# Weight loads in four groups, and the five engine lists ordered anew, in a kernel that runs a one-layer vision tower on one core

## The chip, the core and the metric

The kernel runs on one core of a Trainium2 chip. A core has five engines that run their own instruction streams: TensorE (PE, matmuls; its weight loads are shown as PEld), VectorE (DVE), ScalarE (ACT), GpSimd (POOL), and SyncE (SP), which issues the transfers here. They meet only at semaphores. The metric is the device time of one launch in microseconds, which is the time for all 128 images.

## What is computed

For each of 128 images of 3x224x224: cut into 196 patches of 16x16, take the real part of each patch's 2-D FFT, weight it and project it to 192 numbers; add a class token and positions (197 tokens). Then two residual blocks: attention with 12 heads of 16, and attention with 12 heads of 64 whose queries and keys are normalised per head and whose heads are weighted by gates (2 shared heads, the best 2 of 10 routed heads).

```python
h = tok(x, freq_weight_h, freq_weight_w, proj_w, proj_b, cls_token, pos_emb)
h = h + attn(layernorm(h), Wq, bq, Wk, bk, Wv, bv, Wo, bo)
h = h + ffn(layernorm(h), qkv_w, qkv_b, q_norm_w, ..., wg_w, wg0_w, wg1_w, proj_w, proj_b)
# ffn:
q = layernorm(q, q_norm_w, q_norm_b); k = layernorm(k, k_norm_w, k_norm_b)
o = softmax((q * scale) @ k.T) @ v          # 12 heads of 64
o = masked_gates[..., None] * o
return o @ proj_w + proj_b
```

## The kernel before

An image is a chain of some 58 PE steps, each with its evacuations and pointwise work on DVE, ACT and POOL. The tokens lie in two chunks of 99 partitions. The steps are named in the lists of `ORDER` (lines 145 to 172):

- `tok`: the image, folded by the symmetry of the FFT (`fold`, `xhi`, `xlo` make an fp16 high and low part), times the effective token weights: 22 matmuls.
- `x1T`, `qk1_0..2`, `v1`, `s1_0..11`, `ctx0..2`, `wo`: first attention. `s1` on PE does four heads at once, in a block of 32 rows each; its entry in the list names four banks. `ctx` works in blocks of 32 columns.
- `x2T`, `qk0..5`, `v2_0..3`, `ms0..2`, `rstd0..5`: second attention's projections and head norms. `ms` (mean squares by a selection matrix) has blocks of 32 columns. On POOL, `sq` makes the squares and `bias` adds the norm's bias.
- `s2_0..11`: scores, two heads at once in blocks of 64 rows, fp32. DVE takes the row maxima (`nmax`), ACT the exponentials and their sums, DVE divides the gate by the sum (`gr`), POOL multiplies (`sc`), PE transposes (`pT`, fp32, full array), ACT copies the result, and `o2` multiplies with the values, two heads at once in blocks of 64 columns, fp32. `proj` is the last projection, 36 matmuls.

Each engine has a list of its own, written out by hand. An entry `3:s1_0@4135` reads: in iteration i do step s1_0 of image i+3, and put its results in PSUM banks 4, 1, 3 and 5. `run_phases` walks the list once per iteration, i from -4 to 127, and leaves out the steps of images that don't exist; the middle iterations are a hardware loop. An engine does its list strictly in order; a step that waits holds up everything behind it. A bank has one sequence of users, in the order of PE's list; a step waits (`room_for`) until the user before it has been read out.

Ahead of the lists stand the preparations. SP issues 29 loads of weights and constants, all on one semaphore `s_w` (lines 404 to 428). Many land in buffers that the images use later (`raw(p1, ...)`, `raw(pT, ...)`). DVE waits for all of them (line 824), scales the token weights (signal `s_pw` to PE, which makes the effective token weights in 24 matmuls, lines 533 to 538), subtracts the means of `wq` and `wk`, splits each weight into fp16 parts (`split`, lines 841 to 855), fills buffers (lines 859 to 877), scales PE's product (lines 879 to 885) and signals `s_const` (line 886). POOL waits for that and clears rows of `p1` and `pT` (lines 448 to 453); ACT and PE wait for POOL. Every DVE step here waits for the one before it (`link`).

Of the kernel before, what the change touches and what calls it, by code (L numbers as in the profile page):

```python
# [143 lines left out]

ORDER = {
    "pe": """
0:pT_1@1 0:pT_2@4 0:s2_8@35 2:ctx1@6 1:ms0@0 1:ms1 1:ms2 2:ctx2@2 0:pT_3@1 0:pT_4@7 0:pT_5@3 3:x1T@4 0:o2_0@6 0:o2_1@7
0:s2_10@21 0:pT_6@0 1:rstd0@4 1:rstd1@3 1:rstd2@5 3:qk1_0@6 0:pT_7@0 0:pT_8@4 1:s2_0@32 0:pT_9@7 2:wo@4 0:o2_2@0
0:o2_3@5 1:v2_0@1 1:rstd3@2 0:pT_10@7 0:pT_11@6 3:s1_0@4135 1:s2_2@02 0:o2_4@6 0:o2_5@7 1:v2_1@4 3:qk1_1@1 1:v2_2@3
1:v2_3@6 2:x2T@5 1:rstd4@3 4:tok@4 3:v1@0 3:s1_4@3257 2:qk0@1 2:qk1@0 2:qk2@4 2:qk3@1 3:qk1_2@6 1:rstd5@2 1:s2_4@43  # L150
3:ctx0@0 2:qk4@5 1:s2_6@12 1:pT_0@4 3:s1_8@5760 0:proj@3 2:qk5@7
""",
    "dve": """
1:s2_1 0:gr5 2:wo 0:ol2 0:ol3 1:v2_0 1:rstd3 3:s1_0 3:s1_1 3:s1_2 1:s2_2 3:s1_3 2:nx2 0:ol4 1:v2_1 1:v2_2 1:s2_3
3:qk1_1 1:v2_3 2:x2T 0:ol5 1:rstd4 4:tok 3:s1_4 1:gl 3:ctx0 3:s1_5 1:gate1 3:s1_6 1:gate2 1:gate3 1:gr0 3:s1_7 1:rstd5
1:s2_4 3:cl0 1:s2_5 3:qk1_2 1:gr1 1:s2_6 3:s1_8 3:s1_9 1:gr2 3:s1_10 3:s1_11 0:proj 1:s2_7 3:ctx1 3:ctx2 1:s2_8 4:nx1
1:gr3 1:s2_9 3:cl1 3:cl2 2:var2 1:gr4 4:x1T 1:ol0 1:s2_10 2:rstd0 1:ol1 2:rstd1 1:s2_11 4:qk1_0 2:rstd2 2:s2_0
""",
    "act": """
1:qk0 1:qk1 2:s1_5 1:qk2 2:s1_6 1:qk3 2:qk1_2 2:s1_7 2:ctx0 0:s2_4 1:qk4 0:s2_5 0:pT_0 2:s1_8 2:s1_9 0:s2_6 2:s1_10  # L160
2:s1_11 1:qk5 0:pT_1 0:s2_7 2:ctx1 0:pT_2 0:s2_8 1:var0 2:ctx2 0:pT_3 1:var1 0:pT_4 0:s2_9 3:x1T 0:pT_5 0:o2_0 0:pT_6
0:o2_1 0:s2_10 3:qk1_0 0:pT_7 0:pT_8 0:s2_11 1:s2_0 1:s2_1 0:pT_9 0:o2_2 0:o2_3 0:pT_10 0:pT_11 3:s1_0 3:s1_1 0:o2_4
3:s1_2 4:xhi 3:s1_3 3:qk1_1 0:o2_5 1:s2_2 2:x2T 1:s2_3 3:v1 3:s1_4 1:gate0
""",
    "pool": """
0:sc1 0:bias5 0:sc2 1:sq4 1:sq5 0:sc3 0:sc4 1:bias0 0:h2c 1:h2b 0:sc5 2:root2 1:bias1 4:fold 4:xlo 1:bias2 3:h1b
1:bias3 1:bias4 4:root1 2:sq0 2:sq1 1:sc0 2:sq2 2:sq3
""",
    "sp": """
4:load 0:store  # L170
# [31 lines left out]
def build_vit_block(nc, ins, out, images):  # L202
    with ExitStack() as ctx:
# [200 lines left out]
        loads = [*zip(basis, ("basis0", "basis1", "basis2")), (proj_tok, "proj_tok"), (freq_h[:], "freq_h"), (freq_w[:], "freq_w"),
                 (pos, "pos"), (tok_add, "tok_add"), (wq1_raw, "wq1"), (wk1_raw, "wk1"), (wv1_raw, "wv1"),
                 (wgate_raw, "wgate"), (wq_raw, "wq"), (wk_raw, "wk"), *zip(wv2_raw, ("wv2a", "wv2b")),
                 (ident[:], "ident"), (sel_var[:], "sel_var"), (sel_rstd[:], "sel_rstd"), (low_rows[:], "low_rows"), (weight_rows[:], "weight_rows"),
                 (bias_rows[:], "bias_rows"), (mask1[:], "mask1"), (wo1_raw, "wo1"), (bo1[:], "bo1"),
                 (ln_w[:], "ln_w"), (ln_b[:], "ln_b"), (wp2_raw, "wp2"), (bp2[:], "bp2")]
# [411 lines left out]
        def _(dve):  # L821
            V = nc.vector

            dve.wait_ge(s_w, 16 * len(loads))
# [11 lines left out]
            for x in (wq_raw, wk_raw):  # L836
                link(V.tensor_reduce(wqk_mean[:], x, op=ALU.add, axis=AX.X))
                link(V.tensor_scalar(wqk_mean[:], wqk_mean[:], 1.0 / E2, None, ALU.mult))
                link(V.tensor_tensor(x, x, wqk_mean[:].unsqueeze(3).to_broadcast([128, 3, H, E2]), op=ALU.subtract))
# [32 lines left out]
            for x in (mhalf,):  # L872
                link(V.memset(x[:], -0.5))
            link(V.memset(ones[:], 1.0))
            link(V.memset(gx[:], 2.0))
# [281 lines left out]
```

## Time and profile before

| | |
|---|---|
| median of 3 runs | 5231.84 us (5231.14 to 5232.46) |
| the profiled execution | 5229.47 us, its span 5227.7 us, mean granted clock 0.994 |
| busy, share of the span | PE 5089.4 us (97%), DVE 4644.1 (89%), ACT 4374.0 (84%), POOL 3438.4 (66%) |
| instructions | PE 61744 matmuls, DVE 14799, ACT 17537, POOL 3462 |
| bytes moved | 131.44 MB, a mean of 25 GB/s |
| the chain that ended last | PE 96% |

How to read it: busy time is the time in which an engine's instructions run, without semaphore and register work. Matmuls are pipelined: one begins before the one ahead has ended, and the times between their starts, not their durations, add up to the time of a step. The share of busy time is a mean over the start, the loop and the end. In a timeline, consecutive instructions of one kind are merged into a row: its first column is the start of the first of them, so the difference of the first columns of two rows is the time of everything from the one to the other.

### The profile page before, as it was taken

The numbers are of one execution on the slowest core, as the hardware profiler recorded it, in microseconds if no ns is written. First come the engines' busy times: TensorE is split into PE (matmuls) and PEld (weight loads), VectorE is DVE, ScalarE is ACT, GpSimd is POOL, SyncE is SP. The second block draws the span as 40 slices with busy tenths as digits, with TensorE's granted clock in tenths as the row PEclk, the third lists the DMA queues.
The fourth block names the chain that finished last, engine by engine and source line by source line (L and its number), as shares of the span: only waits on it lengthen the run. The fifth ranks groups of instructions, "written<-read, shape, count | busy, mean of one in ns | idle before, by whom it ended". The sixth has DMA issues, their size and how long they took to land.

```text
span 5227.7 us, 196546 instructions
## 1 busy us (share of the span) xinstructions
PE 5089.4 (97%) x61744; PEld 4233.4 (81%) x61744; DVE 4644.1 (89%) x14799; ACT 4374.0 (84%) x17537; POOL 3438.4 (66%) x3462
## 2 busy tenths in 40 slices
...
GB/s 83 21 24 29 22 22 23 28 22 22 29 22 22 29 22 22 29 22 22 23 28 22 22 29 22 22 29 22 22 29 22 22 23 28 22 22 29 22 23 8
DMA packets 69030, 131.44 MB, mean 25 GB/s; under 512 B 8628, under 2 KB 34624, under 8 KB 68704
## 3 DMA queue, kind: packets, MB, share of 16 engines
...
q14 instruction: 30, 0.25, 0.0%
...
## 4 chain that ended last, share of the span: by engine, by line
PE 96%; issue 2%; ACT 1%; DVE 1%; POOL 0%; POOLq 0%; ACTq 0%; DVEq 0%
PE bank L521 82%; PE bank L698 12%; PE bank L563 2%; ACT p L766 0%; ACT pq L804 0%; DVE nmax L939 0%; POOL pq L505 0%; ACT pT L810 0%; DVE nmax L1038 0%; DVE x L909 0%; DVE qkn L1033 0%; ACT qkc L778 0%; DVE qk L934 0%; DVE v L1015 0%; DVE stats L896 0%
## 5 line engine op out<-in xcount | busy, mean ns | idle before, releaser
L505 POOL TENSOR_TENSOR pq<-pq,gn 99x788 f32<-99x788 f32 x768 | 1152.5, 1501 | 747.3 <-DVE gn L1047 735.1
L766 ACT ACTIVATE p<-bank,nmax 99x197 f32<-99x197 f32 x3072 | 1289.3, 441 | 276.8 <-DVE nmax L939 276.8
L804 ACT ACTIVATE pq<-bank,nmax 99x197 f32<-99x197 f32 x3072 | 1330.0, 464 | 9.3 <-DVE nmax L1038 8.9
L810 ACT ACTIVATE pT<-bank 99x394 f32<-99x394 f32 x1536 | 764.2, 519 | 242.6 <-PE bank L698 242.6
L939 DVE TENSOR_REDUCE nmax<-bank 99x2 f32<-99x394 f32 x1536 | 820.5, 562 | 87.5 <-PE bank L521 59.3
L509 POOL TENSOR_TENSOR sq<-qkc 128x396 f32<-128x396 f32 x768 | 658.6, 872 | 318.4 <-ACT qkc L778 318.4
L1038 DVE TENSOR_REDUCE nmax<-bank 99x2 f32<-99x394 f32 x1536 | 849.4, 560 | 5.2 <-PE bank L521 5.2
L804 ACT ACTIVATION_READ_ACCUMULATOR pq<-bank,nmax 99x1 f32 x3072 | 752.7, 245 | 0.0
L521 PE MATMUL bank<-x2T,wqkc 128*128 128x198 f16 (+1 forms) x7680 | 742.3, 249 | 5.8 <-ACT p L766 4.9
L698 PE MATMUL bank<-ident,pq 99*99 99x99 f32 (+1 forms) x6144 | 723.1, 256 | 3.7 <-POOL pq L505 1.7
L698 PEld LDWEIGHTS bank<-ident,pq 99*99 99x99 f32 (+1 forms) x6144 | 606.2, 165 | 143.8 <-issue 139.8
L521 PEld LDWEIGHTS bank<-x2T,wqkc 128*128 128x128 f16 (+1 forms) x7680 | 646.5, 97 | 80.4 <-issue 41.1
L521 PE MATMUL bank<-qkb 64*99 64x197 f32 x6144 | 703.0, 347 | 5.2 <-issue 3.0
L514 POOL TENSOR_TENSOR qkb<-qkn,ln_b 128x396 f32<-128x396 f32 x768 | 645.1, 848 | 67.7 <-DVE qkn L1033 67.4
L766 ACT ACTIVATION_READ_ACCUMULATOR p<-bank,nmax 99x1 f32 x3072 | 676.6, 220 | 0.0
L521 PE MATMUL bank<-pT,v 128*64 128x197 f32 x6144 | 599.1, 336 | 1.0 <-ACT pT L810 0.9
L521 PEld LDWEIGHTS bank<-qkb 64*99 64x99 f32 x6144 | 451.2, 162 | 126.0 <-issue 83.9
L521 PEld LDWEIGHTS bank<-pT,v 128*64 128x64 f32 x6144 | 406.1, 136 | 116.8 <-issue 32.7
L521 PE MATMUL bank<-wv,x2T 128*99 128x384 f16 (+3 forms) x2560 | 497.6, 333 | 0.2 <-ACT p L766 0.2
L463 POOL TENSOR_TENSOR xl<-xa,xh 128x784 f16<-128x784 f32 x128 | 208.5, 1629 | 370.3 <-ACT xh L738 370.3
L1033 DVE TENSOR_TENSOR qkn<-bank,qkc 128x396 f32<-128x396 f32 x768 | 431.2, 562 | 5.9 <-PE bank L521 0.4
L521 PEld LDWEIGHTS bank<-wv,x2T 128*99 128x99 f16 (+1 forms) x2560 | 294.1, 125 | 146.8 <-issue 73.0
...
## 6 DMA issues: line engine op xcount, KB each, us to landing
xa<-in_xa SPq DMA_DIRECT2D x128, 392.0 KB, 3.1
xb<-in_xb SPq DMA_DIRECT2D x128, 392.0 KB, 3.7
out_tokens<-res SPq DMA_DIRECT2D x128, 74.2 KB
out_tokens<-res SPq DMA_DIRECT2D x128, 73.5 KB
...
```

Source lines behind the costliest of these rows:

```text
L463: nc.gpsimd.tensor_tensor(xl[:, :, 1:T], xa[:], xh[:, :, 1:T], op=ALU.subtract).then_inc(s_xl.up(), 1)
L505: nc.gpsimd.tensor_tensor(pair, pair, factor, op=ALU.mult).then_inc(s_sc.up(), 1)
L509: nc.gpsimd.tensor_tensor(sq[:, t], qkc[:, t], qkc[:, t], op=ALU.mult).then_inc(s_sq.up(), 1)
L514: nc.gpsimd.tensor_tensor(qkb[:, t], qkn[:, t % QKN_SLOTS], ln_b[:].unsqueeze(2).to_broadcast([128, 2, TP]), op=ALU.add).then_inc(s_qk.up( ...
L521: return nc.tensor.matmul(o, l, r, start=first, stop=last)
L698: last = nc.tensor.transpose(o[0:TC, k * T + c * TC:k * T + c * TC + n], pq[0:n, h % SLOTS, c, k * TC:k * TC + TC], ident[0:n, 0:n])
L766: last = nc.scalar.activation(p1[0:TC, h, c, :], psum("s1", h)[0:TC, c * T:c * T + T], ACT.Exp, bias=nmax1[:, c, h:h + 1], accum_out=sum1[ ...
L804: last = nc.scalar.activation(pq[0:TC, h % SLOTS, c, 0:T], psum("s2", h)[0:TC, c * T:c * T + T], ACT.Exp, bias=nmax2[:, h, c:c + 1], accum ...
L810: nc.scalar.activation(pT[0:TC, h].rearrange("p a b -> p (a b)"), psum("pT", h)[0:TC, 0:2 * T], ACT.Copy).then_inc(free("pT", h), 1)
L939: V.tensor_reduce(nmax1[:, :, h], psum("s1", h)[0:TC, 0:2 * T].rearrange("p (a b) -> p a b", a=2), op=ALU.max, axis=AX.X, negate=True).the ...
L1033: V.tensor_tensor(qkn[:, t % QKN_SLOTS].rearrange("p a b -> p (a b)"), psum("rstd", t)[:, 0:2 * TP], qkc[:, t].rearrange("p a b -> p (a b) ...
L1038: V.tensor_reduce(nmax2[:, h, :], psum("s2", h)[0:TC, 0:2 * T].rearrange("p (a b) -> p a b", a=2), op=ALU.max, axis=AX.X, negate=True).the ...
```

## The change

1. The 29 loads are issued in another order, in four groups with a semaphore each: for the token weights (8 loads: the bases, `proj_tok`, `freq_h`, `freq_w`, `bias_rows`, `mask1`), for the first attention (4: `wq1`, `wk1`, `wv1`, `wgate`), `wq` and `wk` (2), and all others (15). PE waits for the first group only.
2. DVE fills its buffers (all but `v2`) before it waits for any load, without a `link` between them. Then it waits for one group at a time: token weights, splits of the first attention's weights, means and splits of `wq` and `wk`, everything else.
3. The lists of all engines but SP are ordered anew. Each holds the same steps as before; positions, numbers of images ahead and banks differ. On PE `s2_8` and `s2_10` stand together, and so do `s2_4` and `s2_6`; `o2_2` and `o2_3` stand apart. The greatest number of images ahead is 4, as before.

The lists, after (those before are printed above):

```diff
     "pe": """
+2:s1_8@6725 0:o2_0@0 0:o2_1@1 0:rstd5@4 1:qk4@3 1:qk5@6 3:x1T@4 0:s2_8@72 0:s2_10@30 1:ms0@6 2:ctx1@5 1:ms1 1:ms2
+2:ctx2@7 0:pT_4@4 3:qk1_0@2 0:pT_5@5 0:pT_6@4 3:v1@1 1:rstd0@6 1:rstd1@3 0:o2_2@5 0:pT_7@6 0:pT_8@2 3:s1_0@4307
+0:o2_3@5 1:rstd2@6 0:pT_9@1 1:v2_0@2 2:wo@4 0:pT_10@3 0:pT_11@2 1:s2_0@61 0:o2_4@3 0:o2_5@0 1:rstd3@4 3:qk1_1@7
+3:qk1_2@5 1:v2_1@3 1:v2_2@4 1:rstd4@6 1:v2_3@1 2:x2T@7 1:s2_2@32 3:s1_4@4056 3:ctx0@1 2:qk0@7 2:qk1@3 2:qk2@4 4:tok@2
+1:s2_4@10 1:s2_6@75 2:qk3@4 1:pT_0@3 1:pT_1@6 0:proj@1 1:pT_2@0 1:pT_3@3
     "dve": """
+0:s2_11 1:var2 0:gr4 3:qk1_0 1:rstd0 2:cl2 1:rstd1 0:ol2 3:s1_0 3:s1_1 0:gr5 3:s1_2 3:s1_3 1:v2_0 1:rstd2 2:wo 0:ol3
+1:s2_0 3:ctx0 1:s2_1 1:rstd3 0:ol4 2:nx2 3:qk1_1 1:v2_1 1:v2_2 1:rstd4 3:qk1_2 0:ol5 1:v2_3 1:s2_2 2:x2T 3:s1_4 1:s2_3
+1:gl 3:s1_5 1:gate1 1:gate2 1:gate3 3:s1_6 3:cl0 1:gr0 3:s1_7 1:s2_4 1:s2_5 1:gr1 4:tok 1:s2_6 1:s2_7 4:nx1 1:gr2
+0:proj 3:s1_8 3:s1_9 3:s1_10 1:rstd5 3:s1_11 3:ctx1 1:ol0 1:s2_8 1:s2_9 4:x1T 3:ctx2 1:gr3 1:ol1 1:s2_10 3:cl1
     "act": """
+0:pT_2 0:pT_3 2:s1_8 2:s1_9 2:s1_10 0:o2_0 1:qk4 2:s1_11 1:qk5 0:o2_1 3:x1T 0:s2_8 0:s2_9 2:ctx1 1:var0 1:var1 0:pT_4
+0:s2_10 3:qk1_0 2:ctx2 0:pT_5 0:s2_11 3:v1 0:pT_6 0:o2_2 0:pT_7 0:pT_8 3:s1_0 0:o2_3 3:s1_1 3:s1_2 0:pT_9 0:pT_10
+0:pT_11 3:s1_3 0:o2_4 0:o2_5 1:s2_0 3:qk1_1 4:xhi 1:s2_1 3:qk1_2 2:x2T 1:s2_2 3:s1_4 3:ctx0 1:gate0 1:s2_3 2:qk0
+3:s1_5 2:qk1 3:s1_6 2:qk2 3:s1_7 1:s2_4 1:s2_5 1:pT_0 2:qk3 1:pT_1 1:s2_6 1:s2_7
     "pool": """
+0:sc4 1:h2b 1:bias0 1:bias1 0:sc5 4:fold 2:root2 4:xlo 3:h1b 1:bias2 1:bias3 1:bias4 2:sq0 2:sq1 1:sc0 1:sc1 4:root1
+1:sc2 2:sq2 2:sq3 1:bias5 2:sq4 1:h2c 2:sq5 1:sc3
```

The preparations, the core of the diff:

```diff
-            for dst, name in loads:
-                sp.dma_start(dst, ins[name]).then_inc(s_w, 16)
+            for dst, name in token_loads:
+                sp.dma_start(dst, ins[name]).then_inc(s_w0, 16)
...
+            for dst, name in last_loads:
+                sp.dma_start(dst, ins[name]).then_inc(s_w3, 16)
-            pe.wait_ge(s_w, 16 * len(loads))
+            pe.wait_ge(s_w0, 16 * len(token_loads))
             pe.wait_ge(s_pw, 1)
-            dve.wait_ge(s_w, 16 * len(loads))
+            V.memset(parts[0][:], 1.0)
+            V.memset(parts[1][:], 1.0)
+            for x in (vs1, ctxT, pq, oT, xh, xl):
+                V.memset(x[:], 0.0)
...
+            dve.wait_ge(s_w0, 16 * len(token_loads))
...
+            dve.wait_ge(s_w1, 16 * len(first_loads))
+            split(wq1_raw, wqk1[:, :, 0:384])
...
+            dve.wait_ge(s_w2, 16 * len(second_loads))
             for x in (wq_raw, wk_raw):
...
+            dve.wait_ge(s_w3, 16 * len(last_loads))
             for x, n, m in zip(wv2_raw, (0, 384), (384, 768)):
...
-            for x in (vs1, ctxT, pq, oT, v2, xh, xl):
-                link(V.memset(x[:], 0.0))
+            link(V.memset(v2[:], 0.0))
```

## Rows read from the trace of the kernel before

**Rows 1.** Windows: stretch, us, then busy us (instructions) by engine, clock, DMA share, GB/s.

```profile
2000.00:3000.00 1000.00, 998.52 (x12203) 831.56 (x12201) 907.14 (x2922) 863.59 (x3466) 678.74 (x685) 1.00 0.07 24
```

**Rows 2.** PE's timeline over one image: start us, us, engine, line, tiles, count.

```profile
2500.93 0.59 PE L698 MATMUL bank<-ident,pq 99*99 99x99 f32 x4
2501.36 0.67 PE L521 MATMUL bank<-rs_hl,sel_rstd 128*128 128x198 f16 x6
...
2502.74 0.86 PE L698 MATMUL bank<-ident,pq 99*99 99x99 f32 x8
2503.53 0.91 PE L521 MATMUL bank<-qkb 64*99 64x197 f32 x8
...
2505.89 1.56 PE L521 MATMUL bank<-pT,v 128*64 128x197 f32 x16
2507.38 1.02 PE L521 MATMUL bank<-wv,x2T 128*99 128x384 f16 x5
...
2508.41 0.86 PE L698 MATMUL bank<-ident,pq 99*99 99x99 f32 x8
2509.32 0.55 PE L521 MATMUL bank<-qk 32*99 32x197 f16 x16
...
2516.08 0.24 PE L521 MATMUL bank<-weff,xh 128*99 128x192 f16 x1
...
2517.81 0.25 PE L521 MATMUL bank<-weff,xl 128*99 128x192 f16 x1
...
2528.06 0.55 PE L521 MATMUL bank<-qk 32*99 32x197 f16 x16
2528.53 3.17 PE L521 MATMUL bank<-wp,oT 128*99 128x192 f16 x36
2531.54 1.03 PE L521 MATMUL bank<-x2T,wqkc 128*128 128x198 f16 x10
...
2536.53 1.29 PE L698 MATMUL bank<-ident,pq 99*99 99x99 f32 x12
2537.66 0.52 PE L563 MATMUL bank<-ident,parts 99*128 99x99 f16 x8
...
2539.59 0.91 PE L521 MATMUL bank<-qkb 64*99 64x197 f32 x8
2540.43 0.59 PE L698 MATMUL bank<-ident,pq 99*99 99x99 f32 x4
```

**Rows 3.** PE's timeline begun inside an o2 visit, at 2538.7 and at 2539.55.

```profile
2538.49 1.17 PE L521 MATMUL bank<-pT,v 128*64 128x197 f32 x12
...
2539.33 0.33 PE L521 MATMUL bank<-pT,v 128*64 128x197 f32 x2
```

**Rows 4.** ACT's timeline: the first softmax half of s1_8.

```profile
2529.23 0.43 ACT L766 ACTIVATE p<-bank,nmax 99x197 f32<-99x197 f32 x1 [0.51 <-DVE nmax L939]
```

**Rows 5.** Timeline of the start; in brackets the engine's idle time before and what ended it.

```profile
28.01 1.19 DVE L834 TENSOR_SCALAR pT<-pT,freq_h,freq_w 72x576 f32<-72x576 f32 x2 [28.01 <-DMA bp<-in_bp]
...
40.02 0.56 DVE L843 TENSOR_SCALAR wqk<-sq 128x768 f16<-128x768 f32 x1
...
54.20 0.56 DVE L843 TENSOR_SCALAR wv<-sq 128x768 f16<-128x768 f32 x1
...
62.39 0.91 DVE L860 MEMSET parts<- 99x1024 f16 x1 [0.28 <-DVE wp L858]
...
64.53 0.23 DVE L861 CAST ident<-ident 128x128 f16<-128x128 f32 x1
...
69.44 0.70 DVE L877 MEMSET vs<- 128x768 f32 x1 [0.23 <-DVE gx L875]
...
77.71 0.36 DVE L881 TENSOR_SCALAR weff<-bank 128x192 f16<-128x192 f32 x1
...
81.20 4.03 POOL L450 MEMSET p<- 32x4728 f32 x1 [80.75 <-DVE lnvar L886]
```

**Rows 6.** Windows of the start, columns as in rows 1.

```profile
10.00:20.00 10.00, 0.00 (x0) 0.00 (x0) 0.00 (x0) 0.00 (x0) 0.00 (x0) 1.00 1.02 414
```

More of the change, by code:

```diff
@@ L146 @@
     "pe": """
[L147 to L151, printed above, removed]
+2:s1_8@6725 0:o2_0@0 0:o2_1@1 0:rstd5@4 1:qk4@3 1:qk5@6 3:x1T@4 0:s2_8@72 0:s2_10@30 1:ms0@6 2:ctx1@5 1:ms1 1:ms2
@@ L152 @@
+2:ctx2@7 0:pT_4@4 3:qk1_0@2 0:pT_5@5 0:pT_6@4 3:v1@1 1:rstd0@6 1:rstd1@3 0:o2_2@5 0:pT_7@6 0:pT_8@2 3:s1_0@4307
+0:o2_3@5 1:rstd2@6 0:pT_9@1 1:v2_0@2 2:wo@4 0:pT_10@3 0:pT_11@2 1:s2_0@61 0:o2_4@3 0:o2_5@0 1:rstd3@4 3:qk1_1@7
+3:qk1_2@5 1:v2_1@3 1:v2_2@4 1:rstd4@6 1:v2_3@1 2:x2T@7 1:s2_2@32 3:s1_4@4056 3:ctx0@1 2:qk0@7 2:qk1@3 2:qk2@4 4:tok@2
+1:s2_4@10 1:s2_6@75 2:qk3@4 1:pT_0@3 1:pT_1@6 0:proj@1 1:pT_2@0 1:pT_3@3
 """,
     "dve": """
-1:s2_1 0:gr5 2:wo 0:ol2 0:ol3 1:v2_0 1:rstd3 3:s1_0 3:s1_1 3:s1_2 1:s2_2 3:s1_3 2:nx2 0:ol4 1:v2_1 1:v2_2 1:s2_3
@@ L155 @@
-3:qk1_1 1:v2_3 2:x2T 0:ol5 1:rstd4 4:tok 3:s1_4 1:gl 3:ctx0 3:s1_5 1:gate1 3:s1_6 1:gate2 1:gate3 1:gr0 3:s1_7 1:rstd5
-1:s2_4 3:cl0 1:s2_5 3:qk1_2 1:gr1 1:s2_6 3:s1_8 3:s1_9 1:gr2 3:s1_10 3:s1_11 0:proj 1:s2_7 3:ctx1 3:ctx2 1:s2_8 4:nx1
-1:gr3 1:s2_9 3:cl1 3:cl2 2:var2 1:gr4 4:x1T 1:ol0 1:s2_10 2:rstd0 1:ol1 2:rstd1 1:s2_11 4:qk1_0 2:rstd2 2:s2_0
+0:s2_11 1:var2 0:gr4 3:qk1_0 1:rstd0 2:cl2 1:rstd1 0:ol2 3:s1_0 3:s1_1 0:gr5 3:s1_2 3:s1_3 1:v2_0 1:rstd2 2:wo 0:ol3
+1:s2_0 3:ctx0 1:s2_1 1:rstd3 0:ol4 2:nx2 3:qk1_1 1:v2_1 1:v2_2 1:rstd4 3:qk1_2 0:ol5 1:v2_3 1:s2_2 2:x2T 3:s1_4 1:s2_3
@@ L158 @@
+1:gl 3:s1_5 1:gate1 1:gate2 1:gate3 3:s1_6 3:cl0 1:gr0 3:s1_7 1:s2_4 1:s2_5 1:gr1 4:tok 1:s2_6 1:s2_7 4:nx1 1:gr2
+0:proj 3:s1_8 3:s1_9 3:s1_10 1:rstd5 3:s1_11 3:ctx1 1:ol0 1:s2_8 1:s2_9 4:x1T 3:ctx2 1:gr3 1:ol1 1:s2_10 3:cl1
 """,
     "act": """
-1:qk0 1:qk1 2:s1_5 1:qk2 2:s1_6 1:qk3 2:qk1_2 2:s1_7 2:ctx0 0:s2_4 1:qk4 0:s2_5 0:pT_0 2:s1_8 2:s1_9 0:s2_6 2:s1_10
-2:s1_11 1:qk5 0:pT_1 0:s2_7 2:ctx1 0:pT_2 0:s2_8 1:var0 2:ctx2 0:pT_3 1:var1 0:pT_4 0:s2_9 3:x1T 0:pT_5 0:o2_0 0:pT_6
-0:o2_1 0:s2_10 3:qk1_0 0:pT_7 0:pT_8 0:s2_11 1:s2_0 1:s2_1 0:pT_9 0:o2_2 0:o2_3 0:pT_10 0:pT_11 3:s1_0 3:s1_1 0:o2_4
@@ L163 @@
-3:s1_2 4:xhi 3:s1_3 3:qk1_1 0:o2_5 1:s2_2 2:x2T 1:s2_3 3:v1 3:s1_4 1:gate0
+0:pT_2 0:pT_3 2:s1_8 2:s1_9 2:s1_10 0:o2_0 1:qk4 2:s1_11 1:qk5 0:o2_1 3:x1T 0:s2_8 0:s2_9 2:ctx1 1:var0 1:var1 0:pT_4
+0:s2_10 3:qk1_0 2:ctx2 0:pT_5 0:s2_11 3:v1 0:pT_6 0:o2_2 0:pT_7 0:pT_8 3:s1_0 0:o2_3 3:s1_1 3:s1_2 0:pT_9 0:pT_10
+0:pT_11 3:s1_3 0:o2_4 0:o2_5 1:s2_0 3:qk1_1 4:xhi 1:s2_1 3:qk1_2 2:x2T 1:s2_2 3:s1_4 3:ctx0 1:gate0 1:s2_3 2:qk0
+3:s1_5 2:qk1 3:s1_6 2:qk2 3:s1_7 1:s2_4 1:s2_5 1:pT_0 2:qk3 1:pT_1 1:s2_6 1:s2_7
@@ L164 @@
 """,
     "pool": """
-0:sc1 0:bias5 0:sc2 1:sq4 1:sq5 0:sc3 0:sc4 1:bias0 0:h2c 1:h2b 0:sc5 2:root2 1:bias1 4:fold 4:xlo 1:bias2 3:h1b
-1:bias3 1:bias4 4:root1 2:sq0 2:sq1 1:sc0 2:sq2 2:sq3
+0:sc4 1:h2b 1:bias0 1:bias1 0:sc5 4:fold 2:root2 4:xlo 3:h1b 1:bias2 1:bias3 1:bias4 2:sq0 2:sq1 1:sc0 1:sc1 4:root1
+1:sc2 2:sq2 2:sq3 1:bias5 2:sq4 1:h2c 2:sq5 1:sc3
 """,
@@ L394, in build_vit_block @@
                   (("tok", 2), ("wo", 2), ("nx1", 2), ("nx2", 2), ("ctx", 3), ("gl", 1), ("gate", 5), ("var", 2))}
-        s_w = ctx.enter_context(nc.semaphore("weights_loaded"))
+        s_w0, s_w1, s_w2, s_w3 = (ctx.enter_context(nc.semaphore(f"weights_loaded_{name}")) for name in ("token", "first", "second", "last"))
         s_const = ctx.enter_context(nc.semaphore("weights_prepared"))
@@ L402, in build_vit_block @@
         block = ctx.enter_context(nc.Block())
[L404 to L409, printed above, removed]
+        token_loads = [*zip(basis, ("basis0", "basis1", "basis2")), (proj_tok, "proj_tok"), (freq_h[:], "freq_h"), (freq_w[:], "freq_w"),
+                       (bias_rows[:], "bias_rows"), (mask1[:], "mask1")]
+        first_loads = [(wq1_raw, "wq1"), (wk1_raw, "wk1"), (wv1_raw, "wv1"), (wgate_raw, "wgate")]
+        second_loads = [(wq_raw, "wq"), (wk_raw, "wk")]
+        last_loads = [*zip(wv2_raw, ("wv2a", "wv2b")), (wo1_raw, "wo1"), (wp2_raw, "wp2"), (ident[:], "ident"), (pos, "pos"),
+                      (tok_add, "tok_add"), (sel_var[:], "sel_var"), (sel_rstd[:], "sel_rstd"), (low_rows[:], "low_rows"), (weight_rows[:], "weight_rows"),
+                      (bo1[:], "bo1"), (ln_w[:], "ln_w"), (ln_b[:], "ln_b"), (bp2[:], "bp2")]
         def run_phases(eng, engine, steps):
@@ L426, in _ @@
         def _(sp):
-            for dst, name in loads:
-                sp.dma_start(dst, ins[name]).then_inc(s_w, 16)
+            for dst, name in token_loads:
+                sp.dma_start(dst, ins[name]).then_inc(s_w0, 16)
+            for dst, name in first_loads:
+                sp.dma_start(dst, ins[name]).then_inc(s_w1, 16)
+            for dst, name in second_loads:
+                sp.dma_start(dst, ins[name]).then_inc(s_w2, 16)
+            for dst, name in last_loads:
+                sp.dma_start(dst, ins[name]).then_inc(s_w3, 16)
             def load(img, _):
@@ L822, in _ @@
             V = nc.vector
-            dve.wait_ge(s_w, 16 * len(loads))
+            V.memset(parts[0][:], 1.0)
+            V.memset(parts[1][:], 1.0)
+            for x in (vs1, ctxT, pq, oT, xh, xl):
+                V.memset(x[:], 0.0)
+            V.memset(mhalf[:], -0.5)
+            V.memset(ones[:], 1.0)
+            V.memset(gx[:], 2.0)
+            dve.wait_ge(s_w0, 16 * len(token_loads))
             prep = [0]
@@ L835, in _ @@
             V.memset(eps[:], LN_EPS).then_inc(s_pw, 1)
[L836 to L839, printed above, removed]
             def split(source, dest):
```

10 lines of the change are left out of this document (4 added, 6 removed).

## The prediction

> **What bounds the kernel now.** I read three views, in this order. First the busy time of a thousand microseconds in the middle [rows 1]: PE is busy 998.52 of 1000 at the full clock (PEclk 1.00, that is 2.4 GHz), DVE 907, ACT 864, POOL 679. Nothing makes PE wait there that is worth the name, so the period of the loop is the length of PE's own instruction stream. Then PE's timeline over one image [rows 2]: the same step, four transposes behind a score step, starts at 2500.93 and again at 2540.43, so one image costs 39.50 us, and 128 of them are 5056 of the 5227.7 us span. The rest, 172 us, is start, filling and emptying. Third the timeline of the start [rows 5]: DVE does nothing until 28.01 (the last weight has landed), then prepares weights until 81.20, and POOL clears two buffers after that before it touches the first image. So the change has two places: what PE's stream costs when the array changes its block shape, and those 81 us.
>
> **Part 1, block shapes in the loop.** Every step of the five lists is still there, once per image; only order, bank numbers and images ahead are new. PE's work is the same 482 matmul records per image, so what can change is the price of the switches between block shapes and PE's waits. The shapes: full array (projections, transposes), 64 rows (s2), 32 rows (s1), 64 columns (o2), 32 columns (ctx, ms).
>
> Prices come from differences of start times in PE's timeline [rows 2].
> - Transposes (pT): one step alone behind s2 takes 2501.36-2500.93 = 0.43; three behind ctx take 2537.66-2536.53 = 1.13. Two more steps add 0.70, so a step is 0.35 and **entering** the full array with pT costs 0.08. Two pT steps ahead of s2 take 2503.53-2502.74 = 0.79: 0.09 for **leaving** the full array.
> - o2: two steps take 2507.38-2505.89 = 1.49. Inside such a visit five pairs of matmuls take 2539.33-2538.49 = 0.84, so 0.168 a pair [rows 3], 1.34 for the eight pairs; a visit to that shape costs 0.15 in all.
> - s2: one step is four pairs of the same 197 columns, 0.67, and takes 2540.43-2539.59 = 0.84: a visit costs 0.17.
> - Entering the full array with fp16 weights: the token step's 21 intervals are 2517.81-2516.08 = 1.73, 0.0824 each; proj has 36 such matmuls, 2.97, and takes 2531.54-2528.53 = 3.01, so 0.04 for weights 99 columns wide. For weights 128 columns wide (rstd, qk) no row isolates it; it lies between nothing and these 0.04, and I take 0.01.
>
> Now the count, from the two PE lists, each read as a ring. Before there are 23 switches: s2 is visited 6 times, o2 3 times, s1 3 times, the 32-column steps 2 times, and the full array 9 times, entered 4 times by pT, 3 times by 99-wide fp16 weights (two v2, proj), 2 times by 128-wide ones (qk). After there are 20: s2 4 times (s2_8 with s2_10, s2_4 with s2_6), o2 4 times (o2_2 and o2_3 are now apart), s1 3, 32 columns 2, full array 7 times, entered twice by pT and 5 times by rstd or qk. Differences: s2 2 x 0.17 = 0.35 less, o2 0.15 more, leaving the full array 2 x 0.09 = 0.18 less, pT entries 2 x 0.08 = 0.16 less, other entries 3 x 0.04 + 2 x 0.01 - 5 x 0.01 = 0.09 less. Sum **0.63 to 0.65 us less per image; I take 0.65**. Bounds: 0.55, if 128-wide weights cost the 0.04 too, and 0.70.
>
> The page "TensorEngine Tiling (Array Packing)" of the Trainium skill (Tiling Modes) says that changing the tiling mode, not just the tile, drains TensorE. Read alone, that makes all switches alike; by it the sum would be an estimated 3/23 of what the switches cost in all (3.5 us), 0.46 us per image instead of 0.65. The rows side against "all alike": an entry is 0.08 or 0.04 by what is loaded.
>
> **Waits.** Before, PE waits about 0.26 us per image. Two pT steps ahead of s1 take 2509.32-2508.41 = 0.91 where ahead of s2 they take 0.79 (0.12 of waiting), one pT ahead of s1_8 starts 0.07 later than its steps explain, and qk3 waits about 0.07 for its bank. In the new list these three places are gone, but others are as tight. The tightest I find is ACT's queue from s1_8 to the copy of pT_5, which o2_2 needs. PE's stretch from the start of s1_8 to o2_2, summed by the prices above, is 11.6 us. ACT starts 2529.23-2528.06 = 1.17 later [rows 2, 4] and has 7 of its 24 softmax steps and 12 of its 37 others to do. ACT is busy 0.864 of 39.50 = 34.1 us per image [rows 1]; 7/24 of that is 9.9, 12/37 is 11.1, and with the dearer softmax steps weighing more I take 10.4. Together 11.6: o2_2 comes between nothing and some tenths late. Similar near-zero margins stand at ms2 (POOL's squares behind h2c), at o2_3 (needs pT_7, only pT_8 and s1_0 lie between) and at ctx0 (its bank is v2_3's, copied by DVE). I take new waits equal to the old 0.26, with bounds 0 and 0.9. DVE's busy 35.8 us per image [rows 1] leaves room under 38.85. Hence the period goes from 39.50 to **38.85**, and over the 127 intervals between 128 images that is 82.6 us less; by the bounds, 115 less (no waits) to almost nothing (0.9 us of waits).
>
> **Part 2, the start.** Before, DVE's work from 28.01 to 81.20 is 53.2 us [rows 5]. Moved ahead of the first wait, into the time in which nothing but loads runs: memsets of parts, 64.53-62.39 = 2.1; vs1 to xl, 77.71-69.44 = 8.3, less v2's, which stays (1564 of 7282 elements a partition, 1.8), 6.5; and three tiny ones, an estimated 0.5 of the 4.9 between 64.53 and 69.44. That is 9.1 us; started at about 1 us they are over by 11, and the loads hide them. What remains is: token scaling 1.2; means of wq and wk, 40.02-28.01 less that 1.2, 10.8; splits of the first group and of wq and wk, 54.20-40.02 = 14.2; and for the last group 62.39-54.20 = 8.2, small steps 4.4, v2's memset 1.8 and the effective weights 81.20-77.71 = 3.5, together 17.9. In all 44.1 us. PE's 24 matmuls of the effective token weights are issued behind the scaling and still end long before DVE asks for them.
> Landing times are not in the trace by group. By their shapes the 29 loads are 8.4 MB; 4.1 of them move between 10 and 20 us at 414 GB/s [rows 6], which leaves 4.3 for the other 18 us, 0.24 MB a microsecond. If they landed in the order of issue, the token group (1.2 MB) would be there at 5 us, the first (2.7 with it) at 11, the second (5.1) at 17. Transfers overlap, so each can only be later; I take 10, 16 and 20. Then DVE does the token scaling by 12 and waits for the first group until 16; the second is there when its splits are done, the last long before its turn: 16 + 14.2 + 10.8 + 17.9 = 58.9, against 81.2: **22.3 us less**. Bounds: 26.3 (no stall behind 12) and 18.3 (first group at 20). POOL's two memsets, 4.03 each [rows 5], still come after the whole preparation, and the first image's fold, split and token step after them; all that shifts along. SP's 29 issues are only re-ordered, and the images' first load stays behind all of them.
>
> **Part 3, filling and emptying.** Depth is 4 images as before. From the token step of an image to the end of its proj PE needs 4 periods and 2531.54-2516.08 = 15.5 us before, 173.5; after, 4 x 38.85 and tok, s2_4, s2_6, qk3, two pT and proj, 8.1 us, 163.5. This latency is paid once, partly compressed in the half-filled iterations. I take half the 10 us, **5 us less**, with bounds 10 less and 5 more.
>
> **Sum.** 22.3 + 82.6 + 5 = 109.9 us less than the profiled execution's own 5229.5 (span 5227.7 and 1.8 around it), 5119.6; the median of the runs, 5231.8, is 2.4 above that execution, so **5122.0 us**, 2.1% less.
>
> **Rivals.**
> - *The waits go entirely* (a period of 38.6): another 0.26 x 127 = 33 us, 5089. For: the lists keep each consumer at least a microsecond behind its producer. Against: the ACT stretch above. Chance 0.2.
> - *More waits, still faster* (0.6 to 1 us more per image than before at ACT's or POOL's tight places): 5190 at 0.8 us of new waits in all (0.54 more than before). For: four margins near zero, in queues that run in order, so that lateness adds up. Chance 0.18.
> - *ACT becomes the bound, slower.* In the stretch from s1_8 to o2_2 the queue runs without rest. Each further microsecond it is late there is a microsecond of the period, since s1_0 and o2_3 behind need ACT as well. Gains to eat are 0.65 + 0.26 per image and 27/127 = 0.21 from the ends, so the point is 1.12 us of waits per image; at 1.5 us the time is 5232 + 0.38 x 127 = 5280. Against: it needs the 10.4 us of that stretch to be 11.5. Chance 0.06.
> - *The groups don't land in order*, so that the token group ends with the last: then only the 9.1 us of memsets are gained at the start, 13.2 less than forecast, 5135. For: all loads stand in one queue and overlap. Against: DVE's wait before ended with the load issued last, bp [rows 5]. Chance 0.06. The page "DMA: Bandwidth & Descriptors" of the Trainium skill (Queues, rings and completion order) says completion is not first-in-first-out per issuing engine; by it this case would be possible, and no row here shows a group's landing.
> - Forecast as summed: chance 0.5.
>
> **How the numbers follow.** The range 5080 to 5190 leaves out the lowest tail of the first rival, the far end of the second and the third. A difference under 0.2% (10 us) cannot be told from none. Faster by more than that: 0.5 + 0.2 + 0.16 + 0.06 = 0.92; within 0.02; slower 0.06.
>
> **What would show it.** In the profile after: equal steps in PE's timeline 38.6 to 39.1 apart; two joined s2 steps taking 1.51, not 1.68; a lone o2 step 0.82; DVE's first memsets before 10 us; POOL's clearing at 55 to 63 us. I am wrong if PE shows idle time before L521 or L698 in the middle, if joined s2 steps still pay inside, or if DVE waits for a load past 25 us.

## The result and the profile after

| | before | after |
|---|---|---|
| median of 6 runs each | 5231.57 us (5230.75 to 5232.56) | 5189.83 us (5185.25 to 5192.94) |
| the profiled execution, its span | 5229.47, 5227.7 us | 5189.76, 5188.0 us |
| busy in 2000 to 3000 us: PE, DVE, ACT, POOL | 998.52, 907.14, 863.59, 678.74 | 989.32, 915.54, 872.46, 680.49 |

After to before: 0.9919, with a 95% interval of 0.9906 to 0.9932. The change saves 41.7 us, 0.8%, where 109.6 were forecast. The time of 5189.83 lies just inside the upper end of the range (5190), and on the second rival ("more waits, still faster", 5190); less than half of the forecast saving came.

The windows of the kernel after, the middle and the start (columns: stretch; busy us and instructions of PE, PEld, DVE, ACT, POOL; clock; DMA share; GB/s), answer to [rows 1] and [rows 6]:

```profile
2000.00:3000.00 1000.00, 989.32 (x12251) 842.30 (x12240) 915.54 (x2931) 872.46 (x3481) 680.49 (x687) 1.00 0.07 24
10.00:20.00 10.00, 8.98 (x28) 9.01 (x29) 6.78 (x17) 0.00 (x0) 0.00 (x0) 1.00 1.02 418
```

PE was 1.5 us from full in that millisecond; now 10.7 are missing, at the same clock. In the start, DVE and PE work while the loads run; in [rows 6] they stood still.

PE's timeline of the kernel after over one image (start us, us, engine, line, tiles, count; in brackets PE's idle time before and what ended it) answers to [rows 2]:

```profile
2501.73 1.58 PE L528 MATMUL bank<-qkb 64*99 64x197 f32 x16
2503.24 0.54 PE L528 MATMUL bank<-sq,sel_var 128*32 128x198 f32 x8
...
2509.01 0.89 PE L528 MATMUL bank<-pT,v 128*64 128x197 f32 x8
2509.83 0.94 PE L705 MATMUL bank<-ident,pq 99*99 99x99 f32 x8
2510.76 0.55 PE L528 MATMUL bank<-qk 32*99 32x197 f16 x16
...
2514.40 0.90 PE L705 MATMUL bank<-ident,pq 99*99 99x99 f32 x8
2515.33 0.91 PE L528 MATMUL bank<-qkb 64*99 64x197 f32 x8
...
2529.84 1.58 PE L528 MATMUL bank<-qkb 64*99 64x197 f32 x16 [0.40 <-DVE ctxT L1060]
2531.35 1.04 PE L528 MATMUL bank<-x2T,wqkc 128*128 128x198 f16 x10
...
2541.05 1.58 PE L528 MATMUL bank<-qkb 64*99 64x197 f32 x16
```

- The joined steps s2_8 and s2_10 begin at 2501.73 and, an image later, at 2541.05: 39.32 us. Over the whole loop the period is 39.316, against 39.50 before and 38.85 forecast.
- The two joined s2 steps take 2503.24-2501.73 = 1.51, the lone o2 step 2509.83-2509.01 = 0.82: the two prices of the forecast, to the digit.
- Two pT steps ahead of s1 take 2510.76-2509.83 = 0.93, ahead of s2_0 2515.33-2514.40 = 0.93, where 0.79 is the price without a wait [rows 2]: 0.14 of waiting in each place. That is the size of the old kernel's waits.
- The new thing is the row at 2529.84. The token step should be followed by s2_4 at once; PE stands still for 0.40 us and waits for DVE's step at L1060.

The place is seen from the waits that belong to that DVE line over the whole span (who waited for it: us, times), and from the page's row of the s2 matmuls (busy us, mean ns; idle before, of which for L1060):

```profile
  PE bank L528: 53.9, 128
...
L528 PE MATMUL bank<-qkb 64*99 64x197 f32 x6144 | 639.4, 340 | 56.4 <-DVE ctxT L1060 51.5
```

Of these 128 waits, 126 are the ones ahead of s2_4, one an image, with 51.5 us, so 0.41 each; the other two stand ahead of s1 steps in the filling. With the part of the restart that isn't idle by the profile, the place costs 0.467 us per image: the token step with what follows up to the first s2_4 matmul takes 2.374 us, and 1.908 in a kernel where the wait is gone (cl0_early, below). 39.316-0.467 = **38.85**, the forecast's period. So one wait is the whole error in the loop: 0.467 x 127 = 59 us.

Who is late? Bank 1, which s2_4 takes, was ctx0's, and is free when DVE has done `cl0` (L1060). DVE's timeline of the kernel after ahead of that step, and POOL's of the same time:

```profile
2527.54 0.16 DVE L1010 TENSOR_TENSOR gpair<-ginv 99x4 f32<-99x4 f32 x1
2527.73 0.79 DVE L1013 SCALAR_TENSOR_TENSOR gfac<-gpair,gx 99x4 f32<-99x4 f32 x1
2528.55 0.18 DVE L1016 TENSOR_TENSOR mg<-gsel,gfac 99x20 f32<-99x20 f32 x1
...
2528.72 0.56 DVE L948 TENSOR_REDUCE nmax<-bank 99x2 f32<-99x394 f32 x1
2529.20 0.41 DVE L1060 SCALAR_TENSOR_TENSOR ctxT<-ctxT,minus_low,bank 128x197 f16<-128x197 f16 x1
```

```profile
2527.65 0.84 POOL L516 TENSOR_TENSOR sq<-qkc 128x396 f32<-128x396 f32 x1 [1.99 <-ACT qkc L785]
```

The step gfac works on 4 elements a partition and takes 0.79 us. It starts 0.08 after POOL's square has started, and ends at 2528.52, just after the square's end at 2528.49 (by the rounded rows; unrounded it is 0.02). It does that in 126 of 128 images, 16 to 20 ns after the square each time; in the other two it starts outside a POOL instruction and takes 0.16, as before. The group of its line in the kernel after, and in the kernel before (duration min/median/max in ns, first and last start):

```profile
L1013 DVE SCALAR_TENSOR_TENSOR gfac<-gpair,gx x128: 161/790/799, 167.1 to 5157.2; 99x4 f32<-99x4 f32 x128
```

```profile
L1004 DVE SCALAR_TENSOR_TENSOR gfac<-gpair,gx x128: 161/165/698, 194.0 to 5196.8; 99x4 f32<-99x4 f32 x128
```

The 0.62 us that gfac takes longer are just more than the 0.467 that PE then waits: without them cl0 would be through before PE asks for its bank.

The start of the kernel after, DVE's and POOL's timelines, answers to [rows 5]:

```profile
1.04 0.91 DVE L831 MEMSET parts<- 99x1024 f16 x1 [1.04 <-PEq L1158]
...
9.56 1.19 DVE L848 TENSOR_SCALAR pT<-pT,freq_h,freq_w 72x576 f32<-72x576 f32 x2 [0.45 <-DMA mask<-in_mask]
...
13.54 0.56 DVE L852 TENSOR_SCALAR wqk<-sq 128x768 f16<-128x768 f32 x1 [2.67 <-DMA p<-in_wgate]
...
20.45 2.55 DVE L864 TENSOR_REDUCE wqk_mean<-p 128x36 f32<-128x2304 f32 x1
```

DVE fills buffers from 1.04, waits until 9.56 for the token group and until 13.54 for the first group, and for no later one: the means of wq and wk (L864) begin at 20.45 without a wait. The last load of their group, wk, is issued at 8.08 and lands 11.0 us later, at 19.1. POOL's clearing (L457) starts at 56.0, where it started at 81.2.

**Where the time went.** PE's first token matmul starts at 68.8 us (94.0 before), that of image 127 at 5043.5 (5083.5), the last matmul ends at 5184.9 (5224.6). So the start is 25.2 us shorter; from the first image's token step to the last one's it is 4974.7 against 4989.5, 14.8 shorter; from there to the end 141.4 against 141.1, 0.3 longer. Of the 14.8 the period gives 127 x 0.184 = 23.4, and 8.6 are given back, 7.0 of them in the first four intervals between token steps (138.4 us together; 131.4 before). Sum 39.7, the difference of the spans.

### The profile page after: what moved, and what is told of

Its sections match the earlier page's. It is cut to its first block, busy times and chain, and to the rows that moved or that the text cites. A ratio compares the mean times of both kernels' runs of the same rounds, so it can differ in the third digit from the quotient of the medians.

```text
span 5188.0 us, 196660 instructions
## 1 busy us (share of the span) xinstructions
PE 5021.8 (97%) x61744; PEld 4268.3 (82%) x61744; DVE 4664.9 (90%) x14799; ACT 4402.2 (85%) x17537; POOL 3434.1 (66%) x3462
## 4 chain that ended last, share of the span: by engine, by line
PE 52%; DVE 35%; issue 11%; DVEq 1%; ACT 0%; POOL 0%; POOLq 0%; ACTq 0%
PE bank L528 42%; PE bank L705 9%; DVE nmax L948 6%; DVE nmax L1047 4%; DVE qkn L1042 4%; DVE v L1024 2%; DVE gfac L1013 2%; DVE qk L943 2%; DVE x L918 2%; DVE oT L1065 2%; DVE h L970 1%; DVE stats L905 1%; DVE ctxT L1060 1%; DVE vs L960 1%; DVE parts L921 1%
## 5 line engine op out<-in xcount | busy, mean ns | idle before, releaser
L811 ACT ACTIVATE pq<-bank,nmax 99x197 f32<-99x197 f32 x3072 | 1287.3, 447 | 137.8 <-DVE nmax L1047 137.8
L1047 DVE TENSOR_REDUCE nmax<-bank 99x2 f32<-99x394 f32 x1536 | 829.8, 561 | 131.0 <-PE bank L528 131.0
L516 POOL TENSOR_TENSOR sq<-qkc 128x396 f32<-128x396 f32 x768 | 644.5, 846 | 364.1 <-ACT qkc L785 364.0
L948 DVE TENSOR_REDUCE nmax<-bank 99x2 f32<-99x394 f32 x1536 | 821.3, 564 | 41.7 <-PE bank L528 38.7
L817 ACT ACTIVATE pT<-bank 99x394 f32<-99x394 f32 x1536 | 740.5, 526 | 66.0 <-PE bank L705 65.9
L811 ACT ACTIVATION_READ_ACCUMULATOR pq<-bank,nmax 99x1 f32 x3072 | 700.7, 228 | 0.0
L528 PE MATMUL bank<-qkb 64*99 64x197 f32 x6144 | 639.4, 340 | 56.4 <-DVE ctxT L1060 51.5
L528 PE MATMUL bank<-pT,v 128*64 128x197 f32 x6144 | 627.9, 338 | 1.7 <-ACT pT L817 1.4
L528 PEld LDWEIGHTS bank<-qkb 64*99 64x99 f32 x6144 | 471.5, 162 | 124.1 <-issue 96.4
L470 POOL TENSOR_TENSOR xl<-xa,xh 128x784 f16<-128x784 f32 x128 | 224.4, 1754 | 431.2 <-ACT xh L745 431.2
L785 ACT ACTIVATE qkc<-bank 128x396 f32<-128x396 f32 x768 | 409.5, 533 | 5.2 <-PE bank L528 5.2
```

The source lines that it names most:

```text
L516: nc.gpsimd.tensor_tensor(sq[:, t], qkc[:, t], qkc[:, t], op=ALU.mult).then_inc(s_sq.up(), 1)
L528: return nc.tensor.matmul(o, l, r, start=first, stop=last)
L785: nc.scalar.activation(qkc[:, t].rearrange("p a b -> p (a b)"), psum("qk", t)[:, 0:2 * TP], ACT.Copy, scale=1.0 / W_SCALE).then_inc(free(" ...
L811: last = nc.scalar.activation(pq[0:TC, h % SLOTS, c, 0:T], psum("s2", h)[0:TC, c * T:c * T + T], ACT.Exp, bias=nmax2[:, h, c:c + 1], accum ...
L817: nc.scalar.activation(pT[0:TC, h].rearrange("p a b -> p (a b)"), psum("pT", h)[0:TC, 0:2 * T], ACT.Copy).then_inc(free("pT", h), 1)
L948: V.tensor_reduce(nmax1[:, :, h], psum("s1", h)[0:TC, 0:2 * T].rearrange("p (a b) -> p a b", a=2), op=ALU.max, axis=AX.X, negate=True).the ...
```

## Experiments

All kernels below were timed beside the kernel before; its median was 5230.43 us beside the first four and 5232.69 beside the other four. Two first ones take the change apart.

**start_only**: the new preparations with the five lists of before.

```diff
     "pe": """
-2:s1_8@6725 0:o2_0@0 0:o2_1@1 0:rstd5@4 1:qk4@3 1:qk5@6 3:x1T@4 0:s2_8@72 0:s2_10@30 1:ms0@6 2:ctx1@5 1:ms1 1:ms2
...
+0:pT_1@1 0:pT_2@4 0:s2_8@35 2:ctx1@6 1:ms0@0 1:ms1 1:ms2 2:ctx2@2 0:pT_3@1 0:pT_4@7 0:pT_5@3 3:x1T@4 0:o2_0@6 0:o2_1@7
...
```

> The four groups and the early fills with the five old lists. My theory (the start gives its 25 us wherever the lists come from, as POOL's first clearing moved from 81.20 to 56.01): 5206 us, the period stays 39.50. Rival (a faster start is partly eaten in the filling, which has its own chains): 5215 or more.

Measured: 5206.41 us, ratio 0.9953 (0.9937 to 0.9970), period 39.50. The start is worth 24.0 us, with POOL's clearing at 55.8 us.

**lists_only**: the new lists with the preparations of before, all loads on one semaphore.

> The new lists with the old preparations. Theory: period 39.32 as in the changed kernel, filling 1.5 us shorter, emptying 7.3 us longer, so 5215 us. Rival (the start's gain and the lists' are not independent, for instance because the ends meet other clock levels): away from 5215 by over 5 us.

Measured: 5213.2 us, ratio 0.9966 (0.9953 to 0.9978), period 39.33. 17.2 and 24.0 make 41.2 of the 41.7 us: the halves add, and what is missing against the forecast is missing in the lists. The time is the expected one, its split isn't: counted between token steps, as above, the first four intervals are 5.3 us longer than before, and from the last token step to the end it is 0.1 longer.

**cl0_early**: cl0 goes ahead of the gate work, so that it can't be late.

```diff
-1:gl 3:s1_5 1:gate1 1:gate2 1:gate3 3:s1_6 3:cl0 1:gr0
+1:gl 3:s1_5 3:cl0 1:gate1 1:gate2 1:gate3 3:s1_6 1:gr0
```

> The changed kernel, only cl0 moved on DVE's list from behind s1_6 to ahead of gate1. Theory (PE's 0.47 us of waiting ahead of s2_4 is for bank 1, which ctx0 holds until DVE's cl0 has read it, and cl0 stands behind the gates): the wait is gone, period 38.85, 5130 us. Rival (the wait moves: gate3, gr0, sc0 come 0.33 us later and pT_0 waits instead, or s2_4's other bank is as late): period 39.1 to 39.3, 5165 to 5190.

Measured: 5285.89 us, ratio 1.0105 (1.0088 to 1.0122), period 40.11: slower than before. A miss, and the most useful one. Its groups of DVE's gate lines in 2000 to 3000 us (busy us, mean ns | idle), and the wait in its PE timeline:

```profile
L1009 DVE TENSOR_TENSOR gsel<-gx,grest 99x20 f32<-99x20 f32 x25 | 20.0, 798 | 0.9
L1013 DVE SCALAR_TENSOR_TENSOR gfac<-gpair,gx 99x4 f32<-99x4 f32 x25 | 4.1, 162 | 0.9
L1017 DVE TENSOR_TENSOR mg<-gx,gfac 99x4 f32<-99x4 f32 x25 | 20.2, 809 | 0.0
```

```profile
2536.03 0.91 PE L528 MATMUL bank<-qkb 64*99 64x197 f32 x8 [0.99 <-issue]
```

The wait ahead of s2_4 is gone, as meant. But cl0's 0.33 us move the gate steps against POOL's squares: gfac is short again, and now two other steps are long, gsel in the first square and mg (L1017) in the second. With twice the delay and s1_6 behind it, the bank that s2_6 takes from s1_6 comes late (ACT's second read of it ends at 2535.85, s2_6 starts at 2536.03): from the first matmul of s2_4 to that of s2_6 it is 1.91 instead of 0.74 us. So the 0.8 us don't belong to gfac but to what starts in POOL's square.

**sq0_later**: DVE's list as in the change; POOL's first square is moved.

```diff
-2:sq0 2:sq1 1:sc0 1:sc1
+2:sq1 1:sc0 2:sq0 1:sc1
```

> The changed kernel, only POOL's sq0 moved behind sq1 and sc0. Theory (gfac of gate3 on DVE takes 0.79 instead of 0.165 us because it starts while POOL's sq0 runs, and ends when sq0 ends): gfac is back at 0.165, cl0 comes 0.62 us sooner, the wait ahead of s2_4 is gone, period 38.9, about 5135 us, if the moved sq0 hits no other DVE step on the path. Rival (gfac is long for another reason, for instance what it waits for): gfac stays at 0.79 and the period at 39.32.

Measured: 5170.79 us, ratio 0.9885 (0.9869 to 0.9902), period 39.18. Its DVE groups in 2000 to 3000 us, and for comparison gn in the kernel after:

```profile
L1056 DVE TENSOR_TENSOR gn<-rsum,mg 99x4 f32<-99x4 f32 x153 | 49.2, 321 | 5.2
...
L1013 DVE SCALAR_TENSOR_TENSOR gfac<-gpair,gx 99x4 f32<-99x4 f32 x26 | 4.2, 162 | 0.9
```

```profile
L1056 DVE TENSOR_TENSOR gn<-rsum,mg 99x4 f32<-99x4 f32 x151 | 24.8, 164 | 5.2
```

With nothing changed on DVE, gfac is back at 0.16 and the token step is followed by s2_4 after 1.909. The mechanism is the one expected; the gain is a third of the expected one (19 us of 55). gn is now held twice an image (mean 321 ns). One of the two is held in gate3_last (below) as well, where PE doesn't wait for it; the other is held by the moved square, which also stands 0.85 us ahead of POOL's second scaling. PE's lost time is not at its transposes: against gate3_last, PE takes 0.14 us more in the joined visit of s2_8 and s2_10 and 0.18 more for the two steps ahead of o2_2, together the 0.32 between the two periods. Which of the moved square's two delays brings them was not tried.

**sq0_halves**: the same square as two instructions of half the columns. This tells a wait for the end of an instruction from a shared bandwidth.

```diff
+                if t == 0:
+                    nc.gpsimd.tensor_tensor(sq[:, t, 0], qkc[:, t, 0], qkc[:, t, 0], op=ALU.mult)
+                    nc.gpsimd.tensor_tensor(sq[:, t, 1], qkc[:, t, 1], qkc[:, t, 1], op=ALU.mult).then_inc(s_sq.up(), 1)
```

> The changed kernel with one difference: POOL's first square of an image (L516, 128 x 396, 0.84 us) is issued as two instructions of 198 columns each, about 0.43 us each, the semaphore on the second. All five lists stay. Theory (a VectorE instruction with both inputs in SBUF that starts while a POOL instruction runs ends only when that one POOL instruction has ended): gfac starts at the same place and now ends with the first half, at about 0.40 us instead of 0.79; cl0 comes about 0.4 us earlier and most of the 0.47 us ahead of s2_4 goes: period about 38.95, time about 5143 (5130 to 5155). Rival (the two engines share bandwidth, so that the slow-down follows the bytes moved at the same time, not instruction bounds): gfac stays near 0.79 us and the time near 5190. Second rival (late gate work is not what holds s2_4): gfac shorter, time still near 5190.

Measured: 5182.46 us, ratio 0.9905 (0.9888 to 0.9921), period 39.26. The time misses the expectation by 39 us. The mechanism is met: gfac ends 0.02 us after the first half, and takes 0.46 instead of the expected 0.40 us because a half takes 0.52, not 0.43. POOL's and DVE's timelines of this kernel:

```profile
2523.54 0.52 POOL L517 TENSOR_TENSOR sq<-qkc 128x198 f32<-128x198 f32 x1 [1.99 <-ACT qkc L789]
2524.01 0.52 POOL L518 TENSOR_TENSOR sq<-qkc 128x198 f32<-128x198 f32 x1
```

```profile
2523.62 0.46 DVE L1017 SCALAR_TENSOR_TENSOR gfac<-gpair,gx 99x4 f32<-99x4 f32 x1
2524.11 0.46 DVE L1020 TENSOR_TENSOR mg<-gsel,gfac 99x20 f32<-99x20 f32 x1
2524.49 0.15 DVE L1021 TENSOR_TENSOR mg<-gx,gfac 99x4 f32<-99x4 f32 x1
```

The first half ends at 2524.06, gfac at 2524.08; the next step, mg, starts inside the second half (its end 2524.53) and ends at 2524.57. Each DVE step is held to the end of the one POOL instruction in which it starts. With a shared bandwidth, gfac would have stayed at 0.79 and mg at 0.18. I had reckoned with the first step only; the second half took the gain back (cl0 is 0.06 us earlier, not 0.4).

**gate3_last**: POOL as in the change; DVE's gate3 (gfac and the two mg) goes behind s1_6 and cl0.

```diff
-1:gl 3:s1_5 1:gate1 1:gate2 1:gate3 3:s1_6 3:cl0 1:gr0
+1:gl 3:s1_5 1:gate1 1:gate2 3:s1_6 3:cl0 1:gate3 1:gr0
```

> The changed kernel with one difference in the DVE list: 1:gate2 3:s1_6 3:cl0 1:gate3 in place of 1:gate2 1:gate3 3:s1_6 3:cl0. cl0 no longer stands behind the lengthened gfac and ends about 1 us earlier; gfac itself then starts after the square has ended. Theory: the wait of 0.47 us ahead of s2_4 goes, and s1_6 is earlier, not later as in cl0_early: period about 38.85 to 38.95, time about 5130 to 5145. Price inside this: the last operations of gate3 may start in POOL's second square and delay gr0 and so the first scaling on POOL by up to 0.4 us; if that reaches PE, period 39.1, time about 5165. Rival (the list is tight everywhere, and each repair is given back by other collisions): 5175 or more.

Measured: **5131.88 us**, ratio 0.9808 (0.9792 to 0.9825), period 38.87. Its DVE and POOL timelines:

```profile
2536.27 0.57 DVE L948 TENSOR_REDUCE nmax<-bank 99x2 f32<-99x394 f32 x1
2536.75 0.41 DVE L1060 SCALAR_TENSOR_TENSOR ctxT<-ctxT,minus_low,bank 128x197 f16<-128x197 f16 x1
2537.08 0.15 DVE L1013 SCALAR_TENSOR_TENSOR gfac<-gpair,gx 99x4 f32<-99x4 f32 x1
...
2537.64 0.62 DVE L1056 TENSOR_TENSOR gn<-rsum,mg 99x4 f32<-99x4 f32 x1
```

```profile
2536.20 0.85 POOL L516 TENSOR_TENSOR sq<-qkc 128x396 f32<-128x396 f32 x1 [1.99 <-ACT qkc L785]
2537.40 0.85 POOL L516 TENSOR_TENSOR sq<-qkc 128x396 f32<-128x396 f32 x1 [0.36 <-ACT qkc L785]
```

Both steps that now start in the first square, at 2536.27 and 2536.75, read PSUM, and take their usual 0.57 and 0.41. gfac starts behind it and is short. A gn is caught by the second square, but PE waits for nothing behind it. PE is busy 998.86 of 1000 us again. One move on one engine gives 58 us; this kernel beats both others.

**gate3_halves**: both remedies together.

> Both differences together (POOL's first square in two halves, and gate3 behind cl0 on DVE). If the collision with the first square is the one cause of the wait ahead of s2_4, the second remedy has nothing left to win: within 8 us of the better of the two alone, not the sum of the two. If they act on different waits the gains add.

Measured: 5130.93 us, ratio 0.9805 (0.9789 to 0.9822), period 38.87: the same as gate3_last. They act on the same wait, which is gone once.

**s2_apart**: the price of a shape change, by putting one back. x1T, eight fp16 transposes on the full array, goes between s2_8 and s2_10.

```diff
-3:x1T@4 0:s2_8@72 0:s2_10@30
+0:s2_8@72 3:x1T@4 0:s2_10@30
```

> The changed kernel with one difference in the PE list: 0:s2_8 3:x1T 0:s2_10 in place of 3:x1T 0:s2_8 0:s2_10, so that the two score steps in 64-row tiles no longer stand side by side, and one change of shape into the tiles and one out of them come back per image. Theory (shape price): by the rows, 0.82 + 0.98 us for two lone steps against 1.51 us for the joined pair, or about 0.27 to 0.30 us per image: period about 39.6, time about 5225 (5215 to 5235). Rival (most of the price lies under waits for DVE and ACT that are there anyway): period unchanged, time 5185 to 5200.

Measured: 5221.8 us, ratio 0.998 (0.997 to 0.999), period 39.57: 0.254 us per image and 32 us in all more than the change. From the first s2_8 matmul over s2_10, without x1T, PE takes 0.846+0.843 = 1.69 instead of 1.51, and the step before them pays 0.09 for leaving the full array. Both are the forecast's prices (0.17 and 0.09). Their sum is 0.27; two of the small waits are 0.02 shorter each, which is most of the difference to 0.254. The wait of 0.40 us ahead of s2_4 stands as before and hides none of it.

## Why the prediction was right and wrong

- **What bounds the kernel** was right: PE's stream. What was added to it or taken from it came through nearly in full: 0.254 of a price of 0.27 us (s2_apart), 0.447 of a wait of 0.467 (gate3_last).
- **Block shapes, 0.65 us per image**: right. The prices of the s2 and o2 visits and of leaving the full array stand in the rows of after and in s2_apart, and the period less the one wait is the forecast 38.85. The 0.01 for entering with 128-wide weights was a choice; the kernel after bears it out: the two rstd5 matmuls behind o2_1 take 0.180 us, and two such matmuls amid their like 2 x 0.087. The sum of all entries was not measured by itself.
- **Waits, "equal to the old 0.26"**: this step failed. Measured are 39.32-(39.50-0.26-0.65) = 0.73 us, by the same reckoning as in the forecast. Of it 0.47 stands in one place, ahead of s2_4; 0.26 are left for all others. The error was not where I looked. Of the four near-zero margins that I named, o2_2 waits 0.02 us, and ms2 and o2_3 show no wait. I had named ctx0 for its own bank, not for who takes ctx0's bank after it. I counted the margin ahead of cl0 with DVE's durations of before, as though a duration belonged to an instruction. Here it belongs to the instruction and to what POOL does when it starts: the order changed gfac from 0.165 to 0.79. The bounds (up to 0.9 us) did hold it, but they stood for the margins that I named, so they held it by luck.
- **The rival "more waits, still faster"** has the right time, 5190, and nearly the right sum of waits (0.8 us against 0.73), but by chance: it put the lateness on ACT and POOL's tight queues, adding up, and it had the filling 5 us shorter. ACT is not short of time: with its list unchanged, gate3_last has the forecast's period. That excludes the rival "ACT becomes the bound" too.
- **The start, 22.3 us less**: right, 25.2 in the trace and 24.0 in start_only, within the bounds of 18.3 to 26.3. My three landing times were too late by little: 9.6 for 10, 13.5 for 16, 19.1 for 20. With 13.5 in place of 16 the sum would have given 24.8.
- **The groups don't land in order**: that rival is out. The first three landed at 9.6, 13.5 and 19.1, in the order of issue, and loads were still running behind the first (418 GB/s from 10 to 20).
- **Filling and emptying, 5 us less**: wrong in sign, 8.9 us more. The end of the last image is no shorter, and the first four token steps are 7.0 us further apart. The kernel with the new lists alone has 5.3 of these 7.0 (136.7 against 131.4); the kernel with the new start alone has 2.3 (133.7), so an earlier start gives a little back as well, which the forecast had at nothing ("all that shifts along"). A half-filled iteration is not PE's stream but a chain of waits, so half of a latency in full periods is no measure of it. The three largest of PE's waits in the same stretch, first before, then after (us in total, times, longest):

```profile
PE bank L521 <- ACT p L766: 13.4, 6, 3.3
PE bank L521 <- DVE qk L934: 6.8, 3, 4.1
PE bank L563 <- DVE parts L913: 6.0, 1, 6.0
```

```profile
PE bank L528 <- ACT p L773: 15.2, 6, 4.7
PE bank L570 <- DVE parts L922: 10.5, 2, 6.0
PE bank L528 <- DVE qk L943: 2.9, 3, 1.5
```

  Waits for `parts`, the transposes' input, are 4.5 us more, the largest rise of one kind. Which position in the lists brings that was not tried; it stays open.

The account: forecast 109.9 less. The wait takes 59.2 of it (0.466 x 127), the filling 13.9, the start gives 2.9: 39.7, the difference of the spans. gate3_last is the forecast kernel without the surprise: 5131.9 against 5122.0. Of the 10 us left, filling and emptying take 11.7 and the loop 2.2; the start gives 3.9.
